# Two transformer layers on one core: projections of the twice normalised rows in three f32r passes, router weights of layer 0 turned by a transfer, copies ahead of maxima

## What is computed

```
xn = layernorm(x)
x  = x + attention0(xn) + ffn0(xn)
xn = layernorm(x)
x  = x + attention1(xn) + ffn1(xn)
```

## Time and profile before

| | |
|---|---|
| median of 3 runs | 1022.2 us (1020.05 to 1024.38) |
| profiled execution | 1020.45 us; its span 1019.1 us |
| busy: PE, PEld | 985.6, 619.2 us |
| busy: DVE, ACT, POOL | 657.1, 507.5, 428.8 us |
| TensorE clock granted | full in all 40 slices |
| steps 2 to 6 | 124.0 us each; PE busy 123.0 of them |
| transfers | 72.78 MB, 71 GB/s over the span |

### The profile page before, as it was taken

One profiled execution on the slowest core, in us unless ns is written; L12 is line 12 of the kernel. 1 busy time (PEld: TensorE's weight loads), 2 busy tenths in 40 slices (PEclk: granted clock), 3 DMA queues, 4 the chain that ended last, 5 costly groups with the idle time before them and its releaser, 6 DMA issues.

```text
span 1019.1 us, 13351 instructions
## 1 busy us (share of the span) xinstructions
PE 985.6 (97%) x4440; PEld 619.2 (61%) x4440; DVE 657.1 (64%) x1553; ACT 507.5 (50%) x1193; POOL 428.8 (42%) x339
## 2 busy tenths in 40 slices
PE   5999989999999999999999999999999999999998
PEld 2665555675656766567655666556665566656655
DVE  4956758587664876658766577756776467624933
ACT  3654673525746266452664536545464544635222
POOL 4865337551084402753036520565206542045333
PEclk9999999999999999999999999999999999999999
DMA  7140310610423003230232302232023220233061
GB/s 271 33 145 1 115 42 1 137 42 11 126 65 91 24 29 111 74 82 22 77 82 73 82 1 95 70 89 62 1 95 86 70 56 10 95 96 83 22 154 34
DMA packets 34564, 72.78 MB, mean 71 GB/s; under 512 B 4544, under 2 KB 5312, under 8 KB 34112
## 3 DMA queue, kind: packets, MB, share of 16 engines
q1 hardware_dynamic: 33072, 69.03, 24.1%
q10 hardware_dynamic: 1424, 2.90, 0.8%
HBM read 69.04 MB, written 2.88 MB: 71 GB/s over the span
## 4 chain that ended last, share of the span: by engine, by line
PE 90%; DVE 5%; issue 2%; ACT 1%; DMA 0%; POOL 0%; DVEq 0%; ACTq 0%; POOLq 0%
PE ps L598 12%; PE ps L701 12%; PE ps L461 9%; PE ps L463 9%; PE ps L462 9%; PE ps L510 6%; PE ps L535 6%; PE ps L523 5%; PE ps L676 3%; PE ps L606 3%; PE ps L485 2%; PE ps L492 2%; PE ps L647 2%; DVE pt L1355 2%; PE ps L456 2%
## 5 line engine op out<-in xcount | busy, mean ns | idle before, releaser
L1106 ACT ACTIVATE wide<-ps 128x512 f32<-128x512 f32 x136 | 81.2, 597 | 220.1 <-PE ps L463 219.5
L1035 ACT ACTIVATE pw<-ps,w_cols 128x512 f32<-128x512 f32 x144 | 98.8, 688 | 108.3 <-PE ps L463 106.2
L1805 POOL TENSOR_TENSOR atc<-atc,wide 128x512 f32<-128x512 f32 x64 | 82.3, 1286 | 148.4 <-DVE atc L1550 148.4
L995 ACT ACTIVATE pw<-ps,nmax 128x256 f32<-128x256 f32 x256 | 118.1, 471 | 41.6 <-DVE nmax L1344 41.5
L598 PE MATMUL ps<-pw,w_w 128*128 128x512 f32 x288 | 135.4, 592 | 0.0
L1787 POOL TENSOR_TENSOR kr<-qks,w_rope 128x512 f32<-128x512 f32 x32 | 43.5, 1360 | 183.0 <-DVE qks L1322 183.0
L1355 DVE COPY pt<-ps 128x512 f32<-128x512 f32 x128 | 83.8, 685 | 31.3 <-PE ps L523 31.0
L461 PE MATMUL ps<-yc,eg 128*128 128x512 f32 x128 | 96.6, 755 | 0.0
L1344 DVE TENSOR_REDUCE nmax<-ps 128x4 f32<-128x1024 f32 (+1 forms) x80 | 79.3, 1008 | 26.7 <-PE ps L510 26.7
L1421 DVE SCALAR_TENSOR_TENSOR pt<-ps,w_cols,wb 128x512 f32<-128x512 f32 x64 | 47.8, 746 | 75.5 <-PE ps L598 50.1
L598 PEld LDWEIGHTS ps<-pw,w_w 128*128 128x128 f32 x288 | 53.7, 189 | 56.0 <-issue 54.0
(11 more groups left out here) (204 smaller groups left out, 2063.1 us busy)
## 6 DMA issues: line engine op xcount, KB each, us to landing
wb<-scratch SPq DMA_DIRECT2D x128, 256.0 KB, 4.0
wb<-scratch SPq DMA_DIRECT2D x32, 512.0 KB, 5.4
wide<-scratch SPq DMA_DIRECT2D x16, 512.0 KB, 5.9
xin<-in_x SPq DMA_DIRECT2D x8, 256.0 KB, 2.8
out<-wide SPq DMA_DIRECT2D x8, 256.0 KB, 2.1
w_w<-in_w ACTq DMA_DIRECT2D x1, 1152.0 KB, 10.8
wb<-in_w SPq DMA_DIRECT2D x1, 1152.0 KB, 12.7
w_ed<-in_ed SPq DMA_DIRECT2D x1, 1024.0 KB, 17.3
```

The source lines that it names most:

```text
L995: m = act.activation(pw[:, u % 2, j, :], ps[:, score_bank(u, par), qt * SEQ:(qt + 1) * SEQ], ACT.Exp, bias=nmax[:, u % 3, j:j + 1], scale= ...
L1035: act.activation(hid[:, n % 4, :], bank(UPS0[n % 2]), ACT.Gelu, bias=cols[:, C_B1 + 2 * e + c:C_B1 + 2 * e + c + 1], scale=1.0).then_inc(* ...
L1805: pool.tensor_tensor(hh[h], hh[h], sgl[:, (c + 1) % 3, :], ALU.mult).then_inc(*HH_POOL.one)
```

## The change

Four things.

1. `zc` becomes two f32r halves. ACT writes the high half and then gain and bias back into the PSUM bank; DVE subtracts for the low half (`z0_low`, `z1_low`). `wqk` (DVE), `wv` and `uvw` (POOL) are split once at the start, out of the memory of `wide`. `project`, `values`, `uv` and `v1` are three passes each. The denominators' load into `wide` waits for the split of `uvw`; `uvw` is loaded earlier.
2. From step 1 on `wr0` is written expert by expert and SP writes it to `scratch0` transposed, one number of four bytes at a time (4096 of them); PE's transposes and ACT's copy of them go.
3. In `attention` both `pt_copy` go ahead of the maxima in every unit.
4. `values` use banks 6 and 3 in steps from 1 on; `turn_z1` goes ahead of `up1(x, 4)`, `z1_cols` ahead of `silu(x, 4)` and of `y1_rows`; on POOL `normalise` goes ahead of `add0`, and from step 2 on the last `rope_turn` behind the last `normalise`.

```diff
+        wide = sb("wide", [P, PAIRS, TOK])
+        wqk_whole, wv_whole = wide[:, 0, :], wide[:, 1, :]
+        uvw_whole = wide[:, 2:4, :].rearrange("p a t -> p (a t)")[:, 0:5 * P]
...
-        zc = sb("zc", [P, TOK])
+        zc = sb("zc", [P, 2, TOK], F32R)
...
-                sp.dma_start(scratch0, wt0[:, :]).then_inc(*SCRATCH0.one)
+                if s:
+                    by_token = bass.AP(tensor=scratch0.tensor, offset=0, ap=[[1, P], [P, E0 * TILES]])
+                    with nc.allow_non_contiguous_dma(reason="a weight of 4 bytes goes to each row"):
+                        sp.dma_start(by_token, wr0[:, :, :].rearrange("p e t -> p (e t)")).then_inc(*SCRATCH0.one)
+                else:
+                    sp.dma_start(scratch0, wt0[:, :]).then_inc(*SCRATCH0.one)
...
             def project(s, p, k):
-                w.wait_ge(LOADED["wqk"], 16)
-                w.wait_ge(*Z0_COLS.at(s))
+                w.wait_ge(*WQK_SPLIT.at(0))
+                w.wait_ge(*Z0_HIGH.at(s))
                 take(k)
-                pe.matmul(bank(k), wqk[:, p * P:(p + 1) * P], zc[:, :],
-                          start=True, stop=True).then_inc(*PROJECTED.one)
+                for part in range(2):
+                    pe.matmul(bank(k), wqk[:, part, p * P:(p + 1) * P], zc[:, 0, :], start=part == 0, stop=False)
+                w.wait_ge(*Z0_LOW.at(s))
+                pe.matmul(bank(k), wqk[:, 0, p * P:(p + 1) * P], zc[:, 1, :],
+                          start=False, stop=True).then_inc(*PROJECTED.one)
...
-                    if u == 2 and second:
-                        turn_weights0(s, score_bank(2, 1))
-                    if u == 3 and s > 1:
-                        turn_weights0(s, score_bank(3, 1))
...
-                    values(n, 1, 3)
-                    values(n, 2, 2)
+                    values(n, 1, 6 if s else 3)
+                    values(n, 2, 3 if s else 2)
...
+                for dst, e in ((zc[:, 0, :], high), (bank(k), done)):
+                    act.activation(dst, bank(k), ACT.Identity, bias=cols[:, b:b + 1],
+                                   scale=cols[:, g:g + 1]).then_inc(*e.one)
...
+            def z0_low(s, k):
+                w.wait_ge(*Z0_COLS.at(s))
+                dve.tensor_tensor(zc[:, 1, :], bank(k), zc[:, 0, :].bitcast(F32), ALU.subtract).then_inc(*Z0_LOW.one)
...
                     pt_copy(s, u, 0)
-                    if u == 0 and s > 1:
-                        maxima(s, 2)
                     pt_copy(s, u, 1)
-                    if 0 < u < UNITS - 2 or u == 0 and s < 2:
+                    if u < UNITS - 2:
                         maxima(s, u + 2)
...
+            def split_uvw():
+                w.wait_ge(LOADED["uvw"], 16)
+                own(pool.tensor_copy(uvw[:, 0, :], uvw_whole))
+                pool.tensor_tensor(uvw[:, 1, :], uvw_whole, uvw[:, 0, :].bitcast(F32),
+                                   ALU.subtract).then_inc(*UVW_SPLIT.one)
```

More of the change, by code:

```diff
@@ L108, in two_layers @@
         cols = weight("cols", [P, COLS])
-        wqk = weight("wqk", [P, HEADS * DH])
-        wv = weight("wv", [P, HEADS * DH])
+        wide = sb("wide", [P, PAIRS, TOK])
+        wqk_whole, wv_whole = wide[:, 0, :], wide[:, 1, :]
+        uvw_whole = wide[:, 2:4, :].rearrange("p a t -> p (a t)")[:, 0:5 * P]
+        for name, whole in (("wqk", wqk_whole), ("wv", wv_whole), ("uvw", uvw_whole)):
+            weights[name] = (whole, A[name])
         rope0 = weight("rope0", [P, 4, SEQ])
@@ L133, in two_layers @@
         rw0 = sb("rw0", [P, 2, E0], F32R)
+        wqk, wv = sb("wqk", [P, 2, HEADS * DH], F32R), sb("wv", [P, 2, HEADS * DH], F32R)
+        uvw = sb("uvw", [P, 2, 5 * P], F32R)
         sgu = sb("sgu", [P, 2, 2, P], F32R)
@@ L643, in uv @@
             def uv(s, c, i, k):
-                w.wait_ge(LOADED["uvw"], 16)
-                w.wait_ge(*Z1_COLS.at(s))
+                w.wait_ge(*UVW_SPLIT.at(0))
+                w.wait_ge(*Z1_LOW.at(s))
                 take(k)
-                pe.matmul(bank(k), uvw[:, c * P:(c + 1) * P], zc[:, :],
-                          start=True, stop=True).then_inc(*UV.one)
+                for part in range(2):
+                    pe.matmul(bank(k), uvw[:, part, c * P:(c + 1) * P], zc[:, 0, :], start=part == 0, stop=False)
+                pe.matmul(bank(k), uvw[:, 0, c * P:(c + 1) * P], zc[:, 1, :],
+                          start=False, stop=True).then_inc(*UV.one)
                 freed[k] = UV_SILU.at(s, i)
@@ L654, in v1 @@
                     tt = 2 * h + t
[L655 to L656 removed]
+                    half, rows = bank(k)[:, t * GE:(t + 1) * GE], slice(tt * P, (tt + 1) * P)
+                    pe.matmul(half, zc[:, 0, rows], uvw[:, 0, 3 * P:5 * P], start=True, stop=False)
+                    pe.matmul(half, zc[:, 0, rows], uvw[:, 1, 3 * P:5 * P], start=False, stop=False)
+                    m = pe.matmul(half, zc[:, 1, rows], uvw[:, 0, 3 * P:5 * P], start=False, stop=True)
                 m.then_inc(*V1.one)
@@ L1592, in attention @@
                         variance0(1)
+                    if u == 4 and second:
+                        z1_low(0, score_bank(4, 1))
                     if u == 6 and second:
@@ L1606, in experts0 @@
                     route1_weights(x)
+                if more:
+                    z0_low(n, 3)
                 weigh0(s, 0)
@@ L1877, in experts0 @@
                     rope_turn(n, 2)
-                normalise(s, 1)
-                add0(s, 3)
-                if more:
+                if s == 0:
                     rope_turn(n, 3)
                 normalise(s, 2)
+                add0(s, 3)
+                normalise(s, 3)
+                if s and more:
+                    rope_turn(n, 3)
                 add0(s, 4)
-                normalise(s, 3)
                 add0(s, 5)
```

85 lines of the change are left out of this document (53 added, 32 removed).

## The result

| | before | after |
|---|---|---|
| median, us | 1022.2 (5 runs, 1020.05 to 1024.38) | **1014.84** (5 runs, 1012.15 to 1020.37) |
| ratio, 95% interval | | 0.9931 [0.9905, 0.9956] |
| profiled execution, its span | 1020.45, 1019.1 | 1016.07, 1014.8 |

What follows compares the result with a forecast made beforehand. PE bounds the kernel, busy 985.6 of 1019.1 us. Terms 12.8 + 0.7 + 3.8 + 2.5 - 0.3 - 1.5 = 18.0 us, from the median 1022.2 to 1004.2 us; range 996 to 1015.

Steps and rivals of the forecast that it cites:

- Products: In projections, values and `uv`, three f32r passes replace a full f32 product: 0.16 us each, 80 counted, 12.8 us gained.
- `v1`: In `v1`, 256 columns, three passes take 0.41 us against 0.43: 0.7 us gained, ends 2.5 gain and 4.4 loss.
- Rival 3: Three passes do not save, through weight changes between passes or `v1` at 0.189 us: 4.4 us lost, 1009; chance 0.09.
- Turns: In steps 1 to 7 four router-weight transposes leave PE, 0.54 us a step: 3.8 us gained.
- Copies: In attention, steps 2 to 7, PE's wait for the second `pt_copy` ends: 2.5 us gained, ends 0 and 3.7.
- The transfer: SP's 4096-piece router write takes 10 us at 40 ns a piece and hides behind the attention: cost nothing.
- rival 2: The transfer is late, 30.5 us at 119 ns a piece, holding DVE before `weigh0`: 54 us lost, 1058; chance 0.09.
- POOL: In experts0, POOL with `normalise` ahead of the adds ends 1 us sooner: nothing taken, 0 to 1 us a step.
- Start and first steps: First projection waits for the low half, cost 0.3 us; waits in step 0's end and step 1 take back 1.5.
- Rival 1: New waits eat half: ACT, DVE loaded, POOL bound in experts0, copies give nothing; 11.6 us less gain, 1015.8; chance 0.12.
- the room that I counted: Each `zc` adds a second ACT pass (0.7 us) and a DVE subtraction (0.68), 16 times: costs nothing, margin 1 us.

Runs made afterwards that it cites:

- run 1: The changed kernel with POOL's old order in experts0 (add0 and rope_turn ahead of normalise) in all steps but step 1: 1005.95 us.
- run 5: The changed kernel with POOL's old order and the router weights turned by PE again: 1010.22 us.
- run 7: The changed kernel with POOL's old order and the maxima of unit 2 ahead of the second copy of unit 0 as before: 1008.72 us.
- run 9: The changed kernel with the third and fourth `wb` load of each step behind the `wide` loads: 1008.87 us.
- run 4: The changed kernel with the router weights of steps 1 to 7 turned by PE again, without the four-byte transfer: 1011.32 us.
- run 11: The changed kernel with POOL's old order in step 0 alone, `uvw` split behind the staged splits, and router weights turned by PE: 1005.2 us.
- run 2: The changed kernel with POOL's old order in step 0 alone: 1007.29 us.
- run 3: The changed kernel with the split of `uvw` on POOL behind the five staged splits: 1011.03 us.
- run 10: The changed kernel with POOL's old order in step 0 alone, `uvw` split behind the staged splits, two `wb` loads behind `wide`: 1001.72 us.
- run 8: The changed kernel with POOL's old order, router weights turned by PE, and `uvw` split behind the staged splits: 1008.7 us.

## Why the prediction was wrong

**Products, 0.16 us each: right.** In the changed kernel the three passes of a product start at 90.02 (two), 90.49, and the next product at 90.72: 0.70 us.

```profile
90.02 0.63 PE L511 MATMUL ps<-wv,zc 128*128 128x512 f32 x2
90.49 0.39 PE L512 MATMUL ps<-wv,zc 128*128 128x512 f32 x1
90.72 0.63 PE L511 MATMUL ps<-wv,zc 128*128 128x512 f32 x2
```

**`v1`, mis-sized, too dear.** I took 0.41 us for three passes, the middle of 0.35 and 0.465. Passes of 256 columns start 0.117 apart, 0.35 for three: a gain of 2.5 in place of 0.7.

```profile
132.94 0.28 PE L678 MATMUL ps<-uvw,zc 128*128 128x256 f32 x1
133.05 0.28 PE L679 MATMUL ps<-uvw,zc 128*128 128x256 f32 x1
133.17 0.28 PE L680 MATMUL ps<-uvw,zc 128*128 128x256 f32 x1
```

The loads stay at 189 ns each and overlap one another (PEld, start us, us); they don't set the pace.

```profile
133.06 0.19 PEld L680 LDWEIGHTS ps<-uvw,zc 128*128 128x128 f32 x1
133.17 0.19 PEld L678 LDWEIGHTS ps<-uvw,zc 128*128 128x128 f32 x1
```

The prediction tied 0.117 to a fast weight load; the trace has the pace without one. (By the rule that I cited, of "TensorE: Matmul & The Clock Gate", Weight-path perf modes, in the Trainium skill, such loads are fast; the record's 189 ns still does not bear that out.) Rival 3 is out.

**Turns, 3.8: too small.** Alone they are 0.71 us a step (runs 1 and 5), not 0.54: 5.0 in seven steps by periods, 4.3 by the medians. Why 0.17 more than PE's own distance was not tried.

**Copies, 2.5: too small,** 3.7 (run 7); by the medians 2.8.

**The transfer, "cost nothing": this step failed.** Its length was not far off, 14.3 to 17.1 us over the steps where I took 11.5, and `wb` was in time, as argued: DVE never waits for a transfer before `weigh0`, so rival 2 is out. But it is not made up as I had it, of 256 pieces at one price: by the engines' records a piece takes 11 ns, under my lower bound of 25, in step 5 they are through after 8.8 us, and 7 us more pass where I took 1.5. What failed is what I concluded from the sentence that the queue it goes ahead of "holds only the `wb` loads and, 20 us later, the denominators". The denominators' write does go out 20.3 us after the transfer, at 639.16; but the `wb` loads, pushed to 634.90, now stand only 4.3 us ahead of it, and it meets DMA engines that are moving 2 MB. I asked whether the moved transfer meets its own reader and not whether the loads that it pushes meet the next transfer's. By run 9 against the change this is worth 6 us. The estimate in the prediction from the Trainium skill's rate ("DMA: Bandwidth & Descriptors", Bandwidth), 43 us for 4096 packets, was too high here by a factor of near three. The Trainium skill's advice (same page, Rules for kernel authors) sets such a transfer against the DMA transpose, which no run here has. Against PE's turns the transfer loses 3.5 us in the change as it is (run 4) and wins 3.5 once `wide` is in time (run 11).

**POOL, "it ends 1 us sooner; nothing taken": the count was right, its condition was left out.** The new order is worth 0.84 us a step (121.78 to 120.94) where `wide` is in time. I counted instructions and not what the first of them waits for, which the change itself made late.

**Start and first steps, 0.3 + 1.5: this step failed too.** By the landmarks it is about 6: 5.2 for the order in step 0 (run 2, landmark 1) and 0.8 for the split of `uvw` (landmark 0). I wrote that the split delays SP's router transfer "by the same, with 7 us to spare". It had them for `wb`; the chain goes on to the denominators and `wide`, which had none once `normalise` went ahead. And one `normalise` more lies ahead of the third `rope_turn`: by count 1.3 us more even with `wide` in time, which fits what run 3 leaves. The clock made it larger: of the 5.2, PE's idle is 3.5, and the stretch at 1.2 GHz 1.7 (4 us at 0.73 and 4 at 0.84 are 1.1 and 0.6 lost).

**The sum.** In the repaired kernel the steady period is 3.3 us under before (120.38 over four steps), and the terms as measured are 11 x 0.16 + 4 x 0.08 + 0.71 + 0.62 = 3.4. Under POOL's old order only 2.6 of them arrive (run 1): POOL is the bound there, and the new order, for which I took nothing, brings the rest. The gains were thus under-counted, 18 forecast, 20.4 measured in run 10; the changed kernel gives 13 of them back, in step 0 and over `wide`. (The medians of runs 2 and 9 alone put these at 7.6 and 6.0; they don't add up exactly, since how late `wide` is differs between executions.) Two errors that partly cancel leave the time just inside the range, by 0.2 us: that is luck. Rival 1 named the right kind (new waits eat half, 1015.8 forecast, 1014.84 measured, chance 0.12) and was right that POOL could become the bound, but the loss came by another way: ACT and DVE had the room that I counted, the copies gave all, and POOL's waits are for a transfer.

**The 1.75 us** between the profiled execution and the median go with the clock. Executions of the kernel before lie at 1019.9 to 1020.3 with a mean clock of 0.999 to 1.000, at 1021.8 to 1022.8 with 0.998, and one at 1024.0 with 0.997. In ten of the fourteen profiles, that of the changed kernel among them, the lower level lies behind the 2.36 us wait in step 1; in that of the kernel before it does not. No profile of one of its executions at 0.998 is kept, so that the 1.75 us lie at this wait is not shown.

## What to carry to other kernels

When a change delays a transfer, follow the queue past that transfer's own reader: ask what the loads behind it will now overlap, and which engine's *first* instruction hangs on that. Two edits that each gain can lose together when one makes a buffer's filling later and the other its first use sooner; a square of four runs shows it, where each removal by itself only shows that something is better out. Look at the first steps as a case of their own: the order that pays 0.8 us a step in the steady state cost 5 us once in step 0. And where a delay differs from step to step, set it beside the steps' lengths: the one trace then tests the cause.

## What was not expected of the hardware

- A wait of PE of 1.85 to 3.95 us (the shortest in run 3) may be followed by about 3.4 us at 1.2 GHz, passes 0.43 us apart; twice as long in run 9. It did not always come: behind the same 2.36 us it came in some executions and not in others, and behind 3.39 us in run 4 the clock stayed at 1.00. One such stretch in step 1 costs some 1 to 2 us (run 1: 1005.04 at a mean clock of 1.000, 1005.7 to 1006.5 at 0.998; from landmark 1 to 2 runs 5 and 8 take 134.8 with it and 133.1 without).
- A transfer of 4096 four-byte pieces to memory let its follower go 14.3 to 17.1 us later. In step 5 the DMA engines' records of the pieces fill 17.9% of that time, 11 ns a piece, and stop 7 us before its end. From two queues at once the pieces came no faster, and an attention that ran through with one queue stood still for 3 to 5 us with two.
- A write of 16 KB let its follower go 1.5 us later on idle DMA engines, and 3.6 to 6.5 us later behind 2 MB of loads.
